# An attention and mixture-of-experts block in split float32: first layers and query/key projections of some steps in halves of 256 columns, and another order of the SBUF tensors

## The reference

```
x = x + attn_block(layernorm(x))      # layernorm, qkv, 16 heads of 16, window of 15 keys, projection,
                                      # then layernorm, fc1 (256 -> 1024), exact gelu, fc2 (1024 -> 256)
x = x + ffn(layernorm(x))
ffn:  main = gelu(x @ W1m + b1m) @ W2m + b2m
      probs = softmax(mean_over_tokens(x) @ w_gate + b_gate); two of 8 experts are chosen per row
      out = alpha * main + (1 - alpha) * sum_k gate_k * (gelu(x @ W1e[k] + b1e[k]) @ W2e[k] + b2e[k])
```

## Time and profile before

| | us |
|---|---|
| median of 3 runs | 1856.29 |
| lowest, highest run | 1855.82, 1857.02 |
| the profiled execution, its time | 1854.73 |
| the profiled execution, its span | 1852.9 |

### The profile page before, as it was taken

How to read it: one execution, slowest core, us unless ns; L and a number is a source line. 1 busy time by engine, 2 the same in 40 slices (tenths; PEclk the granted TensorE clock), 3 DMA queues, 4 the chain that set the end, 5 groups by cost and what they waited for, 6 DMA issues and landing times.

```text
span 1852.9 us, 49302 instructions
## 1 busy us (share of the span) xinstructions
PE 1840.6 (99%) x19591; PEld 1664.4 (90%) x19591; DVE 1371.1 (74%) x2226; ACT 1167.8 (63%) x1832; POOL 870.9 (47%) x788
## 2 busy tenths in 40 slices
PE   8999999999999999999999999999999999999999
PEld 7899898998989989899898999989899898998998
DVE  7777877778777686776868777787777877778644
ACT  6775756657566575665756657566576755657554
POOL 6555271553716437163462624536255271552725
PEclk9999999999999999999999999999999999999999
DMA  4231312203122031220313113131131311203121
GB/s 144 63 91 31 98 58 52 75 30 98 58 69 69 20 104 53 83 61 24 98 46 92 53 34 93 41 97 54 39 89 34 97 58 51 77 29 98 47 64 58
DMA packets 147437, 121.88 MB, mean 66 GB/s; under 512 B 17964, under 2 KB 139784, under 8 KB 147208
## 3 DMA queue, kind: packets, MB, share of 16 engines
q1 hardware_dynamic: 146512, 117.90, 21.9%
q10 hardware_dynamic: 696, 0.83, 0.1%
HBM read 85.52 MB, written 8.39 MB: 51 GB/s over the span
## 4 chain that ended last, share of the span: by engine, by line
PE 97%; DVE 1%; DMA 0%; ACT 0%; issue 0%; POOL 0%; ACTq 0%; DVEq 0%; POOLq 0%
PE psB L261 58%; PE psA L261 28%; PE psA L1272 4%; PE psA L1289 3%; PE psA L1161 2%; PE psA L1311 2%; DMA raw<-in_L_attn_qkv_w 0%; PE psA L1327 0%; DVE smax L745 0%; POOL wf_lo L513 0%; DVE smax L732 0%; DMA xin<-in_L_attn_x 0%; DVE pr L749 0%; ACT hr_hi L988 0%; ACT pT L992 0%
## 5 line engine op out<-in xcount | busy, mean ns | idle before, releaser
L632 DVE TENSOR_TENSOR hr_lo<-hf,hr_hi 128x512 fp32r<-128x512 f32 x512 | 507.4, 991 | 401.4 <-ACT hr_hi L988 401.3
L522 POOL TENSOR_SCALAR chosen_w<-raw 128x512 fp32r<-128x512 f32 x256 | 197.8, 773 | 644.5 <-DMA raw<-in_L_ffn_W2e 385.4
L988 ACT ACTIVATE hr_hi<-hf 128x512 fp32r<-128x512 f32 x512 | 323.9, 633 | 261.7 <-PE psB L261 179.7
L524 POOL TENSOR_TENSOR chosen_w<-raw,chosen_w 128x512 fp32r<-128x512 f32 x256 | 409.0, 1597 | 21.3
L261 PE MATMUL psB<-z_hi,chosen_w 128*128 128x512 f32 x1024 | 371.5, 404 | 0.0
L261 PE MATMUL psB<-chosen_w,hr_hi 128*128 128x256 f32 x2032 | 360.6, 277 | 0.3 <-DVE hr_lo L632 0.2
L261 PEld LDWEIGHTS psB<-chosen_w,hr_hi 128*128 128x128 f32 x2032 | 322.8, 188 | 19.4 <-DVE hr_lo L632 1.0
L984 ACT ACTIVATE hf<-psB,b1x 128x512 f32<-128x512 f32 x256 | 175.1, 684 | 174.6 <-PE psB L261 173.4
L261 PE MATMUL psB<-chosen_w,hr_lo 128*128 128x256 f32 x1016 | 282.1, 278 | 0.0
L261 PEld LDWEIGHTS psB<-z_hi,chosen_w 128*128 128x128 f32 x1024 | 192.3, 188 | 36.0
L261 PE MATMUL psB<-z_lo,chosen_w 128*128 128x512 f32 x512 | 200.1, 391 | 0.0
(11 more groups left out here) (207 smaller groups left out, 4247.7 us busy)
## 6 DMA issues: line engine op xcount, KB each, us to landing
raw<-in_L_ffn_W1e SPq DMA_DIRECT2D x256, 128.0 KB, 2.2
raw<-in_L_ffn_W2e SPq DMA_DIRECT2D x256, 128.0 KB, 2.2
vb<-vs SPq DMA_DIRECT2D x64, 192.0 KB
vb<-vs SPq DMA_DIRECT2D x64, 160.0 KB
out_x<-acc SPq DMA_DIRECT2D x31, 256.0 KB, 2.2
xin<-in_L_attn_x SPq DMA_DIRECT2D x15, 512.0 KB, 3.8
tm<-in_L_ffn_b2e SPq DMA_DIRECT2D x32, 128.0 KB, 3.0
raw<-in_L_attn_fc_w SPq DMA_DIRECT2D x8, 256.0 KB, 3.9
```

Of the source, the lines that this page charges most:

```text
L522: g.tensor_scalar(wx[0][:, :, s, :], raw[:, s, :].rearrange("p (a n) -> p a n", a=2), 1.0, 0.0, ALU.mult, ALU.add).then_inc(w_hi.sem, 1)
L524: g.tensor_tensor(wx[1][:, :, s, :], raw[:, s, :].rearrange("p (a n) -> p a n", a=2), wx[0][:, :, s, :].bitcast(f32), ALU.subtract).then_i ...
L632: v.tensor_tensor(hr[1][:, c % 2, :], hf[:, c % 3, :], hr[0][:, c % 2, :].bitcast(f32), ALU.subtract).then_inc(h_lo.sem, 1)
L988: a.activation(hr[0][:, c % 2, :], hf[:, c % 3, :], ACT.Copy).then_inc(h_hi.sem, 1)
```

## The change

Two things are changed.

1. **Halves.** A new helper both_halves makes a product of 512 moving columns as two of 256: for each k, three matmuls on the first 256 columns, then three on the last 256. project_qk uses it always. chunk_up uses it unless whole is set, which it is in pass 0 and in the 14 slots named in BEHIND. Those are the slots that come behind other work of the slot before (scores, turn, attend, project, transposes).
2. **Addresses.** hr moves ahead of chosen_w, wv and wproj behind it, zT and z3 behind the token-shaped tensors; chosen_w grows from 2 x 2088 to 2 x 2096 float32; the shifts of 96 and 64 bytes go, and one of 64 bytes is put ahead of zT.

```
--- before.py
+++ after.py
@@ allocation
         wm1 = pair("wm1", [P, KD, HID])
+        CW = KD * P + D
+        raw = sb("raw", [P, RING, CW])
+        hr = pair("hr", [P, 2, T])
+        chosen_w = sb("chosen_w", [P, 2, 2 * RING * D + 48], f32r)
         wv = pair("wv", [P, KD, D])
         wproj = pair("wproj", [P, KD, D])
-        raw = sb("raw", [P, RING, CW])
-        WL = 2 * RING * D
-        chosen_w = sb("chosen_w", [P, 2, WL + 40], f32r)
-        zT = pair("zT", [P, KD, T])
-        z3 = pair("z3", [P, KD, T])
         ... (xin, y, sx, acc, tm)
-        shift("second", 96)
+        shift("z", 64)
+        zT = pair("zT", [P, KD, T])
+        z3 = pair("z3", [P, KD, T])
         wf2 = pair("wf2", [P, KH, D])
         wm2 = pair("wm2", [P, KH, D])
-        shift("hr", 64)
-        hr = pair("hr", [P, 2, T])
@@ new helper
+        def both_halves(eng, dst, a, z, k):
+            for h in range(2):
+                cols = slice(h * T // 2, (h + 1) * T // 2)
+                last = three(eng, dst[:, cols], a, [v[:, k, cols] for v in z], k == 0 and h == 0, k == KD - 1 and h == 1)
+            return last
@@ chunk_up(t, kind, m, whole)
-                    last = three(pe, ps[:, m % 2, :], w1[k], [a[:, k, off:off + T] for a in z], k == 0, k == KD - 1)
+                    if whole:
+                        last = three(pe, ps[:, m % 2, :], w1[k], [a[:, k, :] for a in z], k == 0, k == KD - 1)
+                    else:
+                        last = both_halves(pe, ps[:, m % 2, :], w1[k], z, k)
@@ project_qk
-                    last = three(pe, psA[:, bank, :], [w[:, k, col:col + P] for w in wqk], [z[:, k, :] for z in zT], k == 0, k == KD - 1)
+                    last = both_halves(pe, psA[:, bank, :], [w[:, k, col:col + P] for w in wqk], zT, k)
@@ the loop over t and q
+            BEHIND = (0, 1, 2, 5, 6, 7, 8, 9, 11, 12, 13, 15, 17, SPLIT + 9)
-                        chunk_up(t, *ORDER[q])
+                        chunk_up(t, *ORDER[q], whole=t == 0 or q in BEHIND)
```

More of the change, by code:

```diff
@@ L79, in build @@
         wm1 = pair("wm1", [P, KD, HID])
+        CW = KD * P + D
+        raw = sb("raw", [P, RING, CW])
+        hr = pair("hr", [P, 2, T])
+        chosen_w = sb("chosen_w", [P, 2, 2 * RING * D + 48], f32r)
+        wx = [chosen_w[:, :, n * RING * D:(n + 1) * RING * D].rearrange("p a (s n) -> p a s n", n=D) for n in range(2)]
         wv = pair("wv", [P, KD, D])
         wproj = pair("wproj", [P, KD, D])
-        CW = KD * P + D
-        raw = sb("raw", [P, RING, CW])
-        WL = 2 * RING * D
-        chosen_w = sb("chosen_w", [P, 2, WL + 40], f32r)
-        wx = [chosen_w[:, :, n * RING * D:(n + 1) * RING * D].rearrange("p a (s n) -> p a s n", n=D) for n in range(2)]
-        zT = pair("zT", [P, KD, T])
-        z3 = pair("z3", [P, KD, T])
         xin = sb("xin", [P, NT, D])
@@ L1162, in transposes, with chunk_up @@
                 last.then_inc(tr.sem, 1)
-            def chunk_up(t, kind, m):
+            def chunk_up(t, kind, m, whole):
                 if kind == "m":
-                    ps, z, off = psA, zT, 0
+                    ps, z = psA, zT
                     w1 = [[w[:, k, m * P:(m + 1) * P] for w in wf1] for k in range(KD)]
@@ L1170, in chunk_up @@
                 else:
-                    ps, z, off = psB, z3, 0
+                    ps, z = psB, z3
                     w1, _ = chunk_weights(m)
```

## The result

The change made the kernel no faster, but a little slower. The median of 18 runs after is 1858.76 us (1857.06 to 1859.90), that of 18 runs before 1855.64: a ratio of 1.0016, 95% interval 1.0010 to 1.0023. Forecast were 1846.7 us and a range that ends at 1853.5; the time lies 5.3 us above its upper end. The profiled execution of after took 1857.69 us, 2.96 more than that of before; both have a mean granted clock of 1.000. Nine of the 18 executions after have 0.999 instead, and their median is 1859.43 us against 1857.78 of the other nine; under e9 a trace shows what such an execution has in it.

A forecast was written before the change was run, and what follows sets the result against it. TensorE, busy 99%, was taken as the bound, with time to win inside its stream. Gains 6.2 + 0.9 + 1.2 + 0.4 + 1.4 - 0.5 = 9.6 us gave 1845.1, or 1846.7 as median; range 1841.5 to 1853.5.

The forecast's parts named there:

- Item 1: Layer pairs in 15 slots directly behind a second layer: halves cut a pair from 2.746 to 2.720, gaining 6.2 us.
- Items 2 and 3: First layers of slots 3, 4 and 31 behind query/key gain 0.9 us; query/key itself in halves gains 1.2 us.
- Item 4: Other seams, second layer to values and to whole first layers, all taken as distance 64: gain about 0.4 us.
- Item 5: Whole first layers behind other work, 131 slots: losses at the distance-32 seam into second layers vanish, gaining 1.4, at most 3.1 us.
- Item 6: Rest of the whole first layers: steps stay at 0.2291, taken as 0; 3.4 us gained if they fall to 0.2267.
- Item 7: Transposes of slot 16 already wait for tm, so gains of slots 15 and 16 are lost: about -0.5 us.
- A: Rival: 256-column steps lock into 0.118 over slots 18 to 28, 1865 us; 0.08 together with a fixed cost.
- B: Rival: each split product costs a fixed extra, leaving a gain of 4.2, 1852 us; 0.14 shared with D.
- C: Rival: whole first layers get cheaper too, down to 0.2267 a step, gain 14.7, 1841.6 us; chance 0.12.
- D: Rival: VectorE and GpSimd hand-overs become late and absorb half the gain, 1851.5 us; 0.14 shared with B.
- two sentences of the Trainium skill: About 2.5 ns extra per matmul, so 2064 added cost 5.2 us; weight loads take no read bandwidth, so distances cannot matter.

The follow-up runs named there:

- e9: The changed kernel with the small attention tensors back at their positions of the kernel before, modulo 256 bytes; 1858.71 us, ratio 1.0017.
- e1: The kernel before with only the halves added, its addresses kept; 1871.79 us, ratio 1.0089.
- e7: The changed kernel with hr and second weights moved so the seam from first to second layer is 160 modulo 256 again; 1855.24 us, ratio 0.9999.
- e3: The changed kernel with zT and z3 moved 128 bytes further, so first layers have distance 192 modulo 256; 1888.67 us, ratio 1.0178.
- e2: The changed kernel with its new addresses but every product whole, no halves; 1868.65 us, ratio 1.0071.
- e5: The kernel before, no halves, with zT and z3 moved to distance 0 in first layers, query/key, values and project; 1867.02 us, ratio 1.0063.
- e6: The kernel before with zT and z3 moved to distance 0, plus the halves of the changed kernel; 1876.36 us, ratio 1.0111.
- e4: The changed kernel with halves in every slot except those of pass 0; 1864.85 us, ratio 1.0048.
- e8: Against the kernel before: f chunks whole at old distances, m chunks and query/key in halves at distance 64; 1853.50 us, ratio 0.9987.

## Why the prediction was wrong

**Item 1, pairs in quiet slots: right in 12 of 15 slots.** Windows and timeline give 1.36 and 2.720 where 1.36 and 2.72 stood. What failed is that the other slots would follow: 10, 14 and 16, which come soon behind attention work, run their halves at 0.118 and cost 1.407 to 1.420 a layer, where whole ones cost 1.384 to 1.390. In first layers the 12 slots gain 4.0 us and the three lose 1.3; 6.2 stood for all 15, with the seams behind them.

**Items 2 and 3: right for the layers they name.** The first layers of slots 3 and 4 gain 0.2 each and that of slot 31 gains 0.26; query/key gains 1.0 of 1.2. The second layers of chunks 3, 4 and 31 lose more than that (0.8, 0.5 and 0.25), which belongs to item 5.

**Item 4: wrong in sign, and by a slip.** Values and project lose 0.8 together. The prediction says that all seams have 64 after the change; by its own positions (zT and wf2 64, first weights and wv 0) the seams to and from values and project have 0. Modulo 256 they are 0 and 128, and those are the ones that turn the beat over or start the slow one.

**Item 5: wrong, and the larger error.** I read the earlier trace rows as a disorder that dies out, made by the seam of distance 32, and expected 1.4 from taking that seam away. The seam did the opposite of harm. The 0.017 lost in four steps is what it costs a stream in the slow beat to be drawn back into the fast one at that seam (160 modulo 256): in e1, behind slow halves, the first four steps take 0.474 on average, and in e7, behind fast halves and across the same seam, 0.453. In before, 118 of the 164 second layers whose first layer comes behind attention work or transposes start that way (0.469 or more), and 472 of the 476 behind a whole first layer end fast. That the stream came into them in the slow beat is inferred from this, since whole steps show no beat. Without the seam the same four steps take the same 0.47, and the eight behind them are slow as well: a loss of 5.3 where a gain of 1.4 stood. e7 puts the seam back and the second layers go from +5.3 to -0.9.

**Item 6: wrong.** "If only modulo 128 counts, zero" was the branch I took, on the ground that steps at 0 and at 64 cost the same, though no row of before showed a step of 256 at 0. They don't: 0.113 for a step of 256 at 64, 0.120 at 0. Whole steps went from 0.229 to 0.233, and the first layers concerned cost 2.5; e3 takes it back with nothing but 128 bytes. I had put this item between 0 and a gain of 3.4, with no room for a loss, though no row of before showed a 512 at distance 64 modulo 256.

**Item 7 did not come up in pass 7.** There tm is ready at 824.32 + 2.09 = 826.41 and its transposes start at 826.62, 0.21 later instead of 0.08: TensorE came later than before, not earlier.

```profile
824.32 2.09 DVE L771 TENSOR_SCALAR tm<-y,mv,rs 128x256 f32<-128x256 f32 x2 [0.59 <-POOL rs L478]
826.62 1.03 PE L1166 MATMUL psA<-ident,tm 128*128 128x128 f32 x8
```

**The sum.** Forecast was a gain of 9.6. Measured, in the same terms: halves 3.3 and query/key 1.0 gained, small matmuls 1.1 gained (they stood at nothing, with 1 either way), values and project 0.8 lost, whole first layers 2.5 lost, second layers 5.3 lost.

**The rivals.** A was the right mechanism in the wrong place: I looked for the slow beat in slots 18 to 28, because they are the longest even stretch, and that is where it hardly was, since the stream enters them in the fast beat and nothing disturbs it. It sat in chunks 3 to 16 and in the second layer of chunk 31, behind the transposes of slot 32. By its price, 0.0047 a step, 153 more slow second layers of 12 steps are 8.6 us; 3.3 of it come back, since the irregular start behind a seam of 160 and the longer last step are gone. B falls: two halves at distance 64 cost 0.2267, no more than a whole one anywhere here. C falls (0.2325, not 0.2267). D falls too: span less busy time of PE is 12.2 us in after and 12.3 in before. Of the two sentences of the Trainium skill (TensorE: Matmul & The Clock Gate) that the prediction weighed, the runs agree with neither: kernels that differ in addresses alone differ by up to 30 us (e3 and after), and halves in the fast beat cost less than the whole they replace.

As shown I take: the distance sets the cost of a step (e3 against after, e2 and e5 against before, e6 against e1 differ in addresses alone), the halves pay only at 64 and only where they are entered in the fast beat, and the second layers' loss hangs on the seam from first to second (e7). That it is the distance, and not the place of a tensor, is best borne out for 64, at which 256s run fast in products with five different pairs of places, modulo 256; 192 was seen at two pairs and 0 at one only. Open: why the small attention matmuls leave the stream in one beat or the other; behind turn both occur at one and the same seam, 46 and 28 times in e4. The period of 256 bytes is the shortest that fits these runs; a longer one isn't excluded. What in the chip makes the distance count wasn't tested.

## What to carry to other kernels

When a step has two durations at one and the same address distance, look for what enters and what ends the slow one before removing an irregular step: a seam that costs 0.03 us a pair (e7 against after in slots 20 to 27) may be what keeps twelve steps behind it fast. Split or shift only where the stream arrives in the fast beat (here the m chunks and query/key, e8), and don't treat two address distances as equal because they agree modulo a number that no row has tested.

## What the runs showed of the hardware

Start to start, full clock, float32r, distance of next weights to moving data modulo 256 bytes:

| | distance 64 | distance 192 | distance 0 |
|---|---|---|---|
| 256 columns | 0.1133 or 0.118 | 0.118 | 0.120 |
| 512 columns | 0.233 | 0.229 | 0.2265 to 0.233 |

What a seam does to the beat of the product behind it (distance 64 there):

| seam | from fast | from slow |
|---|---|---|
| 64 (e4, first to second layer) | fast 266 of 266 | slow 203 of 204 |
| 160 (e1 and e7, halves to second layer) | fast 277 of 277 (e7) | fast 276 of 278 (e1) |
| 0 (e4, e8, second layer to values or project) | slow 31 of 31 | fast 27 of 27 |
| 128 (e4, values or project to first layer) | slow 28 of 28 | slow 1 of 1 |

None of this shows in a busy share, a wait or the chain: TensorE is busy 99% in before and in after.
